# A transformer block on one core: another order of score and product matmuls on TensorE, four operand loads per head group, and GpSimd normalising sequences 4 to 8

## What is computed

```python
def attention(x, Wq, bq, Wk, bk, Wv, bv, Wo, bo, head_mask):      # x = layernorm(input)
    q = (x @ Wq.T + bq).reshape(b, s, 16, 8)
    k = (x @ Wk.T + bk).reshape(b, s, 16, 8)
    v = (x @ Wv.T + bv).reshape(b, s, 16, 8)
    attn = softmax(einsum('bqhd,bkhd->bhqk', q, k) / sqrt(8)) * head_mask[None, :, None, None]
    return einsum('bhqk,bkhd->bqhd', attn, v).reshape(b, s, 128) @ Wo.T + bo

x = x + attention(layernorm(x), ...)
x = x + moe(layernorm(x), ...)      # shared expert + the two chosen of 8 experts, gelu, 128 -> 512 -> 128
```

## Time and profile before

| | us |
|---|---|
| median of 3 runs | 681.98 (677.87 to 686.18) |
| the profiled execution, its own time | 682.79 |
| its span in the trace | 681.0 |
| TensorE busy | 636.6 (93%) |
| VectorE busy | 498.9 (73%) |
| ScalarE busy | 411.1 (60%) |
| mean granted TensorE clock | 0.937 |

### The profile page before, as it was taken

How to read it: one execution, slowest core, us unless ns; L and a number is a source line. 1 busy time by engine, 2 the same in 40 slices (tenths; PEclk the granted TensorE clock), 3 DMA queues, 4 the chain that set the end, 5 groups by cost and what they waited for, 6 DMA issues and landing times. The chain is left out here.

```text
span 681.0 us, 15669 instructions
## 1 busy us (share of the span) xinstructions
PE 636.6 (93%) x5218; PEld 394.5 (58%) x5218; DVE 498.9 (73%) x1075; ACT 411.1 (60%) x950; POOL 260.7 (38%) x461
## 2 busy tenths in 40 slices
PE   7888999999999999999999989999999999999998
PEld 4444444444444444444444444444689999998966
DVE  6986567897788788788888877952646666666647
ACT  4654556675676676676676676677435555555651
POOL 5303330131063163163163162264665455545510
PEclk7995559999899899899899898999999999999999
DMA  6776122232234212112112211100122222222164
GB/s 191 246 278 217 38 65 55 73 96 78 79 97 111 77 50 64 49 49 60 53 51 57 55 49 49 34 18 21 59 64 67 67 65 63 68 60 66 52 230 157
DMA packets 41127, 57.53 MB, mean 84 GB/s; under 512 B 11002, under 2 KB 24186, under 8 KB 41066
## 3 DMA queue, kind: packets, MB, share of 16 engines
q1 hardware_dynamic: 36746, 47.86, 23.9%
q0 software_dynamic: 4320, 8.89, 3.9%
HBM read 33.66 MB, written 22.52 MB: 83 GB/s over the span
## 5 line engine op out<-in xcount | busy, mean ns | idle before, releaser
L964 DVE TENSOR_REDUCE mx<-ps 128x2 f32<-128x1024 f32 x256 | 309.1, 1216 | 82.7 <-PE ps L1384 81.0
L830 ACT ACTIVATE probs<-ps 128x512 f32<-128x512 f32 x512 | 263.2, 607 | 115.2 <-PE ps L1410 107.9
L1410 PE MATMUL ps<-q_op,k_op 35*128 35x512 f32 x512 | 190.7, 502 | 28.9 <-ACT probs L830 23.4
L1410 PEld LDWEIGHTS ps<-q_op,k_op 35*128 35x128 f32 x512 | 77.7, 194 | 141.1 <-ACT probs L830 99.4
L1424 PE MATMUL ps<-probs,v_op 128*32 128x256 f32 x2048 | 159.2, 429 | 0.0
L1384 PE MATMUL ps<-k_op,q_op 33*128 33x512 f32 x512 | 153.4, 453 | 3.2 <-DVE mx L964 2.4
L888 ACT ACTIVATE probs<-ps,b_cur 128x128 f32<-128x128 f32 x284 | 80.9, 368 | 68.0 <-PE ps L1629 53.8
L1424 PEld LDWEIGHTS ps<-probs,v_op 128*32 128x32 f32 x2048 | 66.8, 119 | 62.9 <-ACT probs L830 26.2
L714 POOL DMA_INDIRECT results<-rest,row_id x71 | 73.2, 1030 | 73.5 <-DVE rest L1265 55.8
L605 POOL DMA_INDIRECT slots<-route_sb,slot_u x64 | 64.4, 1006 | 89.1 <-ACT probs L830 78.3
L1629 PE MATMUL ps<-xn,w_cur 128*128 128x128 f32 x568 | 77.9, 280 | 1.5 <-ACT probs L888 1.2
(11 more groups left out here) (172 smaller groups left out, 536.2 us busy)
## 6 DMA issues: line engine op xcount, KB each, us to landing
q_op<-q_scr SPq DMA_DIRECT2D x128, 64.0 KB, 2.7
k_op<-k_scr SPq DMA_DIRECT2D x128, 64.0 KB, 2.7
w_sb<-in_W SPq DMA_DIRECT2D x18, 256.0 KB
probs<-slots SPq DMA_DIRECT2D x71, 64.5 KB
q_scr<-probs SPq DMA_DIRECT2D x8, 512.0 KB, 4.0
k_scr<-probs SPq DMA_DIRECT2D x8, 512.0 KB, 4.3
k_scr<-probs SPq DMA_DIRECT2D x8, 256.0 KB, 4.6
k_op<-results SPq DMA_DIRECT2D x4, 512.0 KB, 5.1
```

What stands on the lines that cost most here:

```text
L830: nc.scalar.activation(probs[:, i, j, :], ps[:, BANK["key", b, hg, s], :], ACT.Exp, scale=float(D) ** -0.5).then_inc(s_exp, 1)
L964: nc.vector.reduce_max(mx[:, slot % 2, :, p], ps[:, bank:bank + 2, :], AX.X).then_inc(s_max, 1)
L1410: nc.tensor.matmul(ps[:, bank, :], k_op[hg][at:at + rows, j, P * i:P * (i + 1)], q_op[hg][at:at + rows, j, :], start=True, stop=True).then ...
```

## The change

Three edits in one:

1. **TensorE's order.** `ORDER_PE` gives the attention's order for every quad: key score, row pair, two key scores, row pair, key score, two P.V halves (one key tile). `PV_LAG` = 4 halves sets P.V two key tiles back, in every group. `row_scores` begins with the half on the rows that the key score before it didn't use. An extra comes behind the first P.V half of its quad. `out_norm` begins one maximum earlier.
2. **Operand loads.** `load_group` issues 4 DMAs instead of 8, each with 32 rows; the two parts are an outer step of the source address, of stride 0 for Q.
3. **Normalising.** GpSimd normalises sequences 3 to 7 (counted from 0), ScalarE only 1 and 2.

```diff
-        N_LD, N_SH = 8, 2
+        N_LD, N_SH = 4, 2
...
-        PV_AT = ((3, 3, 4, 5), (2, 3, 4, 5))
+        ORDER_PE = "KRKKRKHH" * (2 * NT)
+        PV_LAG = 4
...
                 for half in range(2):
                     head, at = J * hg + JH * half, ROW_HALF * half
-                    for r in range(PARTS):
-                        for scr, op, first in ((q_scr, q_op, 0), (k_scr, k_op, D * r)):
-                            src = scr[b, :, :].rearrange("(x h) t -> x h t", h=H)[first:first + PR, head:head + JH, :]
-                            sp.dma_start(op[hg][at + PR * r:at + PR * (r + 1), :, :].bitcast(f32), src).then_inc(s_ld[hg], 16)
+                    for scr, op, shift in ((q_scr, q_op, 0), (k_scr, k_op, D)):
+                        seq = scr[b, :, :]
+                        src = bass.AP(tensor=seq.tensor, offset=seq.offset + head * S,
+                                      ap=[[shift * H * S, PARTS], [H * S, PR], [1, JH * S]])
+                        to = op[hg][at:at + KR, :, :].bitcast(f32).rearrange("x j t -> x (j t)")
+                        sp.dma_start(to, src).then_inc(s_ld[hg], 16)
...
+            normalise(POOL_SEQ)
+            ln1_rstd(3)
+            zero_scores(3)
+            normalise(POOL_SEQ + 1)
+            nc.gpsimd.memset(v_op[:, :, :, :, :], 0.0).then_inc(s_pad, 1)
...
+            for b in range(POOL_SEQ + 2, B):
+                normalise(b)
+            max_split(0)
...
-                if b + 2 < B and b + 2 != POOL_SEQ:
+                if b + 2 < POOL_SEQ:
                     normalise(b + 2)
...
-                        if p >= 4 and hg == 2:
-                            out_norm(b, 0, p - 4)
-                        elif p >= 4 and hg == 0 and not first:
-                            out_norm(b - 1, 1, p - 4)
+                        if 3 <= p < 7 and hg == 2:
+                            out_norm(b, 0, p - 3)
+                        elif 3 <= p < 7 and hg == 0 and not first:
+                            out_norm(b - 1, 1, p - 3)
...
-                for half in range(2):
+                for half in (first, 1 - first):
...
+            def attend(b, two):
+
+                g = b * HG + 2 * two
+                key, row, half, due = 0, 0, 2 * NT * g - PV_LAG, None
+                for op in ORDER_PE:
+                    if due is not None and op == "K":
+                        more(*due)
+                        due = None
+                    if op == "K":
+                        at = b, 2 * two + key // (J * NT), key % (J * NT)
+                        key_scores(*at)
+                        key, due = key + 1, at
+                    elif op == "R":
+                        for s in (2 * (row % PAIRS), 2 * (row % PAIRS) + 1):
+                            if (b, 2 * two + row // PAIRS, s) in ROWS:
+                                pair = ROWS[b, 2 * two + row // PAIRS, s]
+                                row_scores(pair // (HG * PAIRS), pair // PAIRS % HG, pair % PAIRS, key % 2)
+                        row += 1
+                    else:
+                        product_half(half)
+                        half += 1
+                        if due is not None:
+                            more(*due)
+                            due = None
```

More of the change, by code:

```diff
@@ L503, in _ @@
             ln1_rstd(2)
[L504 to L516, removed]
+            normalise(POOL_SEQ)
[3 more added lines that the diff above has]
+            nc.gpsimd.memset(v_op[:, :, :, :, :], 0.0).then_inc(s_pad, 1)
+            pool.wait_ge(s_pad, 2)
+            for hg in range(HG):
+                nc.gpsimd.memset(v_op[:, hg, :, :, HALF_OUT * (hg % 2):HALF_OUT * (hg % 2) + 1], 1.0).then_inc(s_pad, 1)
+            for b in range(POOL_SEQ + 2, B):
+                normalise(b)
+            max_split(0)
             def gather_v(b, hg):
@@ L631, in add_bias @@
                     pool.wait_ge(s_xnv, 1)
-                    pool.wait_ge(s_xn, B - 2)
+                    pool.wait_ge(s_xn, POOL_SEQ - 1)
                 sl = x_sb[:, b * NT:(b + 1) * NT, :]
@@ L1348, in transpose_x @@
                     pe.wait_ge(s_xnv, 1)
-                elif b == POOL_SEQ:
-                    pe.wait_ge(s_xnp, 1)
+                elif b >= POOL_SEQ:
+                    pe.wait_ge(s_xnp, b - POOL_SEQ + 1)
                 else:
-                    pe.wait_ge(s_xn, b if b < POOL_SEQ else b - 1)
+                    pe.wait_ge(s_xn, b)
                 wait(pe, s_xnT, b)
@@ L1374, in project_v, with row_scores @@
                 last.then_inc(s_vp, 1)
-            def row_scores(b, hg, p):
+            def row_scores(b, hg, p, first=0):
                 j, i, rows = p // NT, p % NT, KR + 1
@@ L1428, in pv, with product_half @@
                     last.then_inc(s_pv, 1)
-            def products(b, hg, quad):
-                for i in range(NT):
-                    if PV_AT[(hg - 1) % 2][i] == NT + quad and b * HG + hg > 0:
-                        for half in range(2):
-                            pv((b * HG + hg - 1) // HG, (hg - 1) % HG, i, half)
-                for i in range(NT):
-                    if PV_AT[hg % 2][i] == quad:
-                        for half in range(2):
-                            pv(b, hg, i, half)
+            def product_half(n):
+                if 0 <= n < NG * 2 * NT:
+                    g, i = n // (2 * NT), n // 2 % NT
+                    pv(g // HG, g % HG, i, n % 2)
             def max_rows(b, hg):
@@ L1563, in _, with more @@
-            sequences(attend)
-            for i in range(NT):
-                if PV_AT[(HG - 1) % 2][i] >= NT:
-                    for half in range(2):
-                        pv(B - 1, HG - 1, i, half)
+            def more(b, hg, s):
+                for kind, *which in extras(b, hg, s):
+                    if kind == "mx":
+                        max_rows(*which)
+                    elif kind == "project":
+                        project_out(*which)
+                    elif kind == "yT":
+                        transpose_y(*which)
+                    elif kind == "logitsT":
+                        logits_by_expert(*which)
+                    elif kind == "logits":
+                        logits_out(*which)
+                    else:
+                        ranks(*which)
@@ L1569, in _ @@
+            for b in range(B):
+                for two in range(HG // 2):
+                    attend(b, two)
+            for n in range(NG * 2 * NT - PV_LAG, NG * 2 * NT):
+                product_half(n)
             pe.wait_ge(s_wffn, 16 * N_WFFN)
```

27 lines of the change are left out of this document (removed).

## The result

The changed kernel takes 750.1 us (median of 4 runs, 733.6 to 762.6), the kernel before 679.9 beside it (4 runs, 675.3 to 686.2). The ratio is 1.088, with a 95% interval of 1.068 to 1.109; it is taken from the faster runs of each kernel alone (733.6 and 742.7 us of the changed one), which is why it is smaller than 750.1 / 679.9. I had forecast 692 us and a range of 668 to 735.

What follows compares the result with a forecast made beforehand. TensorE's work at 1.2 GHz bounds groups 0 to 2; no engine is full in groups 3 to 29. 682.8 + 20.0 + 2 - 4 - 6.4 - 1.5 = 692.9, less 0.8 for the median: 692 us, range 668 to 735.

Steps and rivals of the forecast that it cites:

- Prologue, +20.0: Before the attention: slower group loads queue ahead of stores, so the attention starts near 71.6 us instead of 51.58.
- Groups 0 to 2, +2 and -4: Attention's first groups: +2 us for stores and a load on two engines, -4 for less time at the low clock.
- the end I had put at 0: Groups 0 to 2: one bound of the clock term, the low stretch starting again with the attention; the other was -12 us.
- Groups 3 to 29, 12.3 and 13.3 us: Group time bound by loads, 13.3 in nine groups with expert weights; 341.1 us in all against 347.5, -6.4.
- the chain of load and shift rows: Each of groups 3 to 29: load issue to landing 12.9 us, less 1.1 of lead, shift rows behind it; 12.2.
- The last two groups, -1.5: End of the attention: these groups lose their short low-clock stretch, 1.5 us less.
- The clock of groups 3 to 29, put at nothing: Groups 3 to 29: no time was added for new stretches at 1.2 GHz.
- The eight short stretches at the low clock: Stretches of some 3.4 us at 1.2 GHz, seven in groups 3 to 29; should mostly go with P.V in all quads.
- my own loads term: Group loads on two DMA engines at 25 GB/s each: 10.4 us a group, TensorE waiting once a group.
- the one with the load on 16 engines (644 us): Rival for the group loads: they still get 16 engines, groups 3 to 29 gain 34 us; chance 0.08.
- The one with slower engines (755 us): Rival for the group loads: 21 GB/s an engine, load 12.5 us, groups 14.4 and 15.4; chance 0.13.
- the order's gain at 1.2 GHz: New TensorE order in groups 0 to 2: TensorE's work is the same at that clock, so nothing changes.

Runs made afterwards that it cites:

- e1: Changed kernel with the eight operand loads of the kernel before, new order and GpSimd normalising kept: 662.7 us, kernel before 683.4; 643.1 against 665.3 on another chip.
- e4: Kernel before with only TensorE's new order and the earlier out_norm; its own loads and normalising: 664.2 us, kernel before 683.4.
- e6: e1 with TensorE also waiting for a small transfer at the start of eight groups: 676.3 us, kernel before 665.8.
- e2: Kernel before with only the operand loads changed to four: 734.1 us, kernel before 683.4.
- e8: e1 with nine and eight unused filler matmuls at the two waits of group 0: 637.7 us, kernel before 665.8.
- e16: The same kernel as e8 on another chip: 669.6 us in eight runs, kernel before 680.4.
- e10: Changed kernel with two unused filler matmuls at each group's start, loads still on two engines: 719.3 us, kernel before 684.6.
- e17: e1 with two unused filler matmuls at the start of groups 0 to 6 alone: 638.7 us, kernel before 665.3, ratio 0.965.
- e18: e1 with one unused filler matmul at the start of groups 0 to 6 alone: 636.9 us, kernel before 665.3, ratio 0.960.

## Why the prediction was wrong

Against the profiled execution my sum was 692.9, and 762.6 came, 69.7 more. That execution is the slowest of the four, so the clock's term below is at its largest. By its terms:

- *Prologue, +20.0*: right. 72.29 instead of 71.6, so +0.7 on the sum.
- *Groups 0 to 2, +2 and -4*: 54.36 us where 51.2 was forecast, +3.1. The low stretch did start again with the attention, the end I had put at 0. I had it begin before the attention; TensorE was back at 2.4 GHz from 69.0 to 72.4 us, and the clock fell right behind a wait of 1.58 us for the first shift rows.
- *Groups 3 to 29, 12.3 and 13.3 us*: the ten of them without any low clock took 13.14 in the mean, 354.8 for 27, so +13.7. Where the load isn't the bound, the order does about what I said: 11.8 us for e1's groups at 2.4 GHz against 11.6. But the chain of load and shift rows was longer than my 12.3: for group 21 from 383.2 to 397.4, 14.2 us, against 12.9 + 0.44. This term is mis-sized, but by itself it would have left the time within the range.
- *The last two groups, -1.5*: nothing gained, +2.0 with the end.
- *The clock of groups 3 to 29, put at nothing*: this is the step that failed. I wrote "The eight short stretches at the low clock should mostly go, since P.V is now spread over all quads, and the 11.6 supposes that", and had no term for new ones. They did go, as e1 and e4 show (1.00 to the end of the attention), but the waits that my own loads term forecast brought seven longer stretches, and the opening one reached 69 us into group 3 and beyond: 405.0 - 354.8 = 50.2 us. By the two group times, 13.1 and 16.9, the seven (146.8 us) are about 33 of it and the opening one's tail about 15. In the fastest run, 733.6 us, the same sum leaves some 21 us for this term if the other terms are alike there, an estimate, since that run has no trace. The rows had the hint: the opening stretch of 51 us came behind a wait of 2.06 us, and I priced a wait of 0.7 to 1.7 us a group (12.3 and 13.3 against 11.6) by its own microseconds alone.

So the mechanism of the loads was right in place and some 14 us short in size; its second effect was missing. The Trainium skill has the effect ("TensorE: Matmul & The Clock Gate", section "HAM oscillation — how this bites in real kernels": a wait for a DMA re-throttles TensorE, again in every tile). What the traces here show differs in size: there waits of 3 to 5 us are each followed by about 1.7 us at the low clock, here 7 to 38 us at 1.2 GHz while TensorE is busy all the time stand behind waits of 0.45 to 2.4 us; the measurement decides.

Of the rivals, the one with the load on 16 engines (644 us) is what e1 built: 662.7 and 643.1 on two chips. The one with slower engines (755 us) has a time near the result by another way: its 21 GB/s was wrong, the window shows 26. I also put the order's gain at 1.2 GHz at nothing; a quad there went from 4.55 to 4.13 us, and a group at 1.2 GHz now takes 16.9 where group 2 took 17.6.

Sizes by themselves: loads alone +50.7 us, order alone -19.2, together +70.2. That is 39 more than their sum (the last on another chip, and the executions' clocks differ). I take the reason to be that the order's shorter groups turn the load's chain from a cover into a wait, and the wait into a low clock: 9 waits against 2, 270 us at 1.2 GHz against 181.

What stays open: which waits of 0.5 to 1.7 us are followed by a stretch (four of seven in e6, six of nine at the group starts of the changed kernel), what sets its length (3 to 38 us), whether the transfers on two engines have a part of their own (e2), and what begins and ends the opening one. The same kernel on the same chip shows it short or long, and e8 against e16 shows how four runs on one chip can mislead.

## What to carry to other kernels

Count the DMA engines that a transfer will get before merging it: half as many issues on two engines instead of 16 cost 51 us here, without the new order. When a change makes TensorE wait even 1 or 2 us once a stage, price the time at 1.2 GHz that follows as well as the wait: here 11 us of waits at group starts went with 147 us at 1.2 GHz, some 33 us of time. And read the granted clock of every run beside its time: 0.01 of it is 5 us in this kernel, more than most edits bring, and only runs on one chip, many of them, tell such edits apart.

## What was not expected of the hardware

- At 1.2 GHz a TensorE that is busy nearly without a gap (49.54 of 50.00 us from 100 to 150 in the changed kernel) did not return to 2.4 GHz for up to 123 us, with matmuls of 33 and 35 rows and of 32 columns. With one or two matmuls of 128 rows and 128 columns at the start of each of the first seven groups or more the opening stretch was 14 to 17 us in three kernels (e10, e17, e18).
- The same kernel on the same chip had a clock of 0.868 to 0.976 (e16, eight runs, 658.1 to 714.1 us).
- A matmul of 128 x 512 on plain f32 operands of this kernel took 0.88 us at 2.4 GHz in two records, where a key score's step is 0.23 to 0.34 us.
